# Two MoE layers on one core: the down biases move from matmuls to the copy out of PSUM, the first seventeen expert tiles take rounded products, and every engine's order is new

## Chip, cores and metric
The kernel runs on one core of one Trainium2 chip. The metric is device time in microseconds (us). Before the change the median of three runs is 795.2 us (793.75 to 796.96).

## What is computed
The input is x of 16 sequences of 256 rows of 128. Layer 0 is attention with 16 heads of 8, and then a mixture of experts. Layer 1 is a gated recurrence with a gated hidden layer, and then a channel mix. The change is in the mixture of experts, which is, with xf the 4096 rows:

```python
scores = jax.nn.sigmoid(xf @ gate_w + bias)
top_scores, top_idx = jax.lax.top_k(scores, 2)          # of 8 experts
top_scores = top_scores / (sum(top_scores) + 1e-06)
up = einsum('th,ehi->tei', xf, up_w) + up_b             # 128 -> 512
eo = einsum('tei,eih->teh', gelu(up), down_w) + down_b  # 512 -> 128
combined = einsum('teh,te->th', eo * 0.1, w)
shared = (gelu(xf @ sw_up + sb_up) @ sw_down + sb_down) * 0.1
out = shared + combined
out = out / (max(abs(out), -1) + 1e-06)
```

## The kernel before
The 4096 rows are eight chunks of 512. All engines run hand-ordered programs that meet at semaphores. `schedule()` (from L308) makes jobs, each a list of stages; two strings, ORDER1 and ORDER2, say in pairs of characters which job issues its next stage. `arrange` walks them, hands out the PSUM banks and buffers of the rings, and puts `fill` stages (short matmuls on constants, L855) where its model of costs (HELD, BEHIND, LANDS) finds TensorE idle too long. Each engine then issues its own stages in the order of the one list, and each waits in that order: what stands behind a waiting instruction waits too.

The work has four parts.
- **Attention**, chunks and sequences interleaved (ORDER1). Its stages among others: `mxm`/`mxr` (row maxima: TensorE L952, VectorE L1290), `atm` (L975, L977), `pv` (L990, L992). In it the layer norm and the routing of a chunk follow its attention, and GpSimd scatters the chunk's rows to the experts' places in HBM (`scatter`, L1935, four stages a chunk; each waits until the one before has landed).
- **First list** (ORDER1): 17 tiles of 256 rows of one expert, which the routing of six chunks already fixes. SyncE's `fetch` reads the tile's expert and row from a table into registers and issues three DMAs, up weights WU (L2044), down weights WD (L2045) and rows XT (L2049), into one of six buffers; from the seventh tile it waits for the last down product of the tile six back. TensorE transposes the rows (`xt`, L1065), VectorE copies them to XS (L1517), four `up` products in float32 follow (L1079; one float32 product is two instructions in the trace), ScalarE's gelu (L1784), four `down` stages of two products each (L1098), VectorE's copy out `ev` (L1539), and GpSimd's `store_rows` (L1946).
- **Second list** (order written out in `schedule`): 22 tiles. VectorE rounds WU to float32r (`wsh`, L1528) and GpSimd takes the rest (`wsl`, WO, L1941); VectorE makes XH and XL of the rows likewise (L1519, L1521). An `up` is then three float32r products WH·XH, WO·XH, WH·XL (L1085 to L1087).
- **Last part** (ORDER2): GpSimd gathers each chunk's two rows per token (`gather`, L1963, each stage after the landing of the one before), VectorE combines (`cmb`, L1548), normalizes (`fin1`, L1570), TensorE transposes (`fin2`, L1113), and layer 1 follows for all chunks interleaved. The shared expert's `up` and `down` for chunk 0 stand at the start of the first list, those of chunks 1 to 7 here.

The down biases are applied with the shared expert's product: `rows` transposes each chunk's routing weights with a column of ones (TensorE L1057, four products; ScalarE L1772 copies them to WT), and the shared expert's last `down` adds four products of WT with the nine bias rows DB (L1105). `ev` of the shared expert (L1535) copies the sum out.

Of the kernel before, what the change touches and what calls it, by code (L numbers as in the profile page):

```python
# [7 lines left out]
F = mybir.dt.float32  # L8
R = mybir.dt.float32r
B16 = mybir.dt.bfloat16  # L10
ALU = mybir.AluOpType
# [27 lines left out]
def constants():  # L39
# [48 lines left out]
    "up": ("PE", 0.858, None), "rows": ("PE", 0.436, None), "down": ("PE", 0.888, None), "ev": ("DVE", 0.6, None),  # L88
    "gelu": ("ACT", 0.57, "gelu"), "t_up": ("PE", 0.434, None), "t_gelu": ("ACT", 0.36, "gelu"), "t_down": ("PE", 0.444, None),
    "t_ev": ("DVE", 0.33, None), "xt": ("PE", 0.218, None), "xs": ("DVE", 0.334, None), "store_rows": ("POOL", 0.55, None),  # L90
# [16 lines left out]
BEHIND = {"PE": 0.165, "ACT": 0.115, "DVE": 0.08, "POOL": 0.045, "SP": 0.0}  # L107
LANDS = {"gather": 2.5, "scatter": 2.5, "fetch": 3.0}
# [6 lines left out]
def cost(name, key):  # L115
# [7 lines left out]
    if name == "down" and key[0] == "s" and key[2] == 3:  # L123
        held = 1.776
# [6 lines left out]
    "AAAAACABAFAAABADAAAAABAEABAGAGABAAAAAKABALABAAAKAGALABAIAAAJAGAAAIAJAGAAABAHAAAIAGAHAGANAIAGAMANANABAMANAMAHABATAHAMABAP"  # L131
    "ATAHAPAQAGAQAHAOAHAOARASAHARAVBBAUASBABBApAoAXAYBABBAYAWBABBAWAYBDAYBAAXBEBDBCBEBFBCAXBFBGAXAWAXBGAWAZAXAWAZAYAWAZAsAZAY"
    "AZArAZArAtAaAqAtAqAcAbAcAtAsAhAbAiAsAtAqAqAhAtAtArAiAgArAhAqAgArAsAiAqAfAdAgAfAsArAGAdAsAfBHAuAHAIAdBHAwAeAwAGBIA1BJAGAv"
    "B1AIAvAIAkB1AIAeBNBKBNBLAkA1AeBKA0A0BNA1BNAyAjAkBLA0AyA2BNA2AjBNAyAzAjAxA2AzAmBcBdAlAmBLBKAlAzBMBLB1AnAxBKB1A4AnBMAIAnAx"
    "B3AnBMB3A4BMA3A4B4BKB4B5BKB5B6BMB6BLBMA3BLBgA3BfBfA6BhBOBeBhBQBgBQBPBeBVBWBVBPB0A6BWBSBVB0BSA5BWBUA5BfB0BhBfBSBTBUA7B0Bh"
    "BeBfA7BRBTBeA7BUBfB2BRA7BgBeBTB2B9BgA8BRBeBgB8BhBgAHBhBXA8BiBYBXAHBYBXAHBjBYBkBjA8BkCBA8BnBoCBCAB+A8B-CABaA8BnB-BoBZBnBq"
    "BaA-BqBZB-BoB+BpA-BmB-BpBbBqB+CABbB+CBBpBmBlCBCQBbCRBsCABmBlBbCpBsBlCpB+BsCAB+CBCpBrCACpB-CBCTBrB-CrBrCTCVCsCrCCBuCVCsCE"
    "CDCECtCDCUCtBuCJCICJCUCuCSCoCuCSCJCIA9CoCIBtCoA9CHA9BtCKCHCoCTA9BvCVBvCUCGCKCHCVCqCTCGBvCKCUCTCqCGCFBvCxCVCwCUCVBwCFCUCS"
# [171 lines left out]
def schedule():  # L310
# [126 lines left out]
    def plan(n):  # L437
# [3 lines left out]
        if n:  # L441
            yield stage("plan_rows", after=[("woh", NB - 1)])
# [48 lines left out]
    def shared_out(c):  # L491
        yield stage("ev", "s", c, after=[("down", "s", c, 3)])
# [1606 lines left out]
```

## Time and profile before

| | us |
|---|---|
| median of three runs | 795.2 |
| the profiled execution | 796.7 |
| its span in the trace | 795.0 |
| TensorE busy | 730.2 |
| VectorE busy | 502.4 |
| ScalarE busy | 498.3 |
| GpSimd busy | 387.8 |

The profile's mean granted TensorE clock is 0.971 of full speed. Starts and stretches in the text are us from the start of the span. By the trace the attention ends at about 360, the first list runs to 448, the second to 528, and the last part to the end. Matmul records overlap, since their ends are modelled: what a stage costs TensorE is read from start to start.

### The profile page before, as it was taken

What the parts mean: (1) busy time and instruction counts of PE and PEld (TensorE: products, weight loads), DVE (VectorE), ACT (ScalarE), POOL (GpSimd) and SP (SyncE); (2) the same over time, 40 slices, a digit from 0 to 9 for tenths busy, and PEclk for the clock granted to TensorE, in tenths of its full rate; (3) what the DMA queues carried; (4) which work ended last, traced back from release to release, by engine and by line L of the source; (5) the groups of instructions that cost most, each with busy time, mean ns of one, the idle gap of its engine ahead of it and who ended that gap; (6) DMA issues with size and microseconds to landing.
All of it is one profiled execution on the core that took longest, in us unless ns stands there. A gap on an engine that the chain in (4) does not pass through costs nothing.

```text
span 795.0 us, 12566 instructions
## 1 busy us (share of the span) xinstructions
PE 730.2 (92%) x3768; PEld 442.7 (56%) x3768; DVE 502.4 (63%) x1906; ACT 498.3 (63%) x749; POOL 387.8 (49%) x563
## 2 busy tenths in 40 slices
PE   4889899899889998988999899998999999999994
PEld 3444445444544544446789899986545644434442
DVE  3387888879984889784912345513346495795652
ACT  1749675775838556655455455552688886688563
POOL 7327444664856277653451355534445465522243
PEclk9999998999999989899999999998999999999998
DMA  9990000000000000005767667711000101000012
GB/s 280 380 369 29 1 1 0 18 12 14 14 24 4 2 28 24 3 15 168 231 214 214 179 204 233 208 40 31 26 25 23 31 22 32 20 1 0 1 40 66
DMA packets 59855, 64.18 MB, mean 81 GB/s; under 512 B 6474, under 2 KB 42668, under 8 KB 59788
## 3 DMA queue, kind: packets, MB, share of 16 engines
q1 hardware_dynamic: 53410, 49.84, 20.3%
q0 software_dynamic: 6320, 13.53, 5.4%
q8 instruction: 30, 0.49, 0.3%
q14 instruction: 37, 0.30, 0.1%
q10 hardware_dynamic: 58, 0.02, 0.0%
HBM read 35.18 MB, written 28.18 MB: 80 GB/s over the span
## 4 chain that ended last, share of the span: by engine, by line
PE 61%; DVE 15%; issue 8%; POOL 6%; ACT 6%; DMA 3%; SPq 0%; DVEq 0%; POOLq 0%; ACTq 0%
PE PS L1098 11%; DVE JK L1290 6%; PE PS L1079 4%; PE PS L952 3%; PE PS L990 3%; PE PS L1161 3%; PE PS L895 3%; PE PS L1154 3%; PE PS L1168 2%; PE PS L901 2%; POOL got L1963 2%; PE PS L907 2%; DMA got<-expert_out,IG 2%; PE PS L975 2%; PE PS L961 2%
## 5 line engine op out<-in xcount | busy, mean ns | idle before, releaser
L1290 DVE CUSTOM_DVE_ANT_0 JK<-PS,CM 128x256 bf16<-128x256 f32 (+1 forms) x512 | 148.9, 352 | 23.3 <-PE PS L952 21.9
L1784 ACT ACTIVATE GF<-PS,XN 128x256 f32<-128x256 f32 x156 | 73.7, 475 | 67.1 <-PE PS L1087 37.4
L1098 PE MATMUL PS<-WD,GF 128*128 128x128 f32 x624 | 94.9, 276 | 0.9 <-ACT GF L1784 0.6
L952 PE MATMUL PS<-KZ,QS 128*128 128x512 f32 x192 | 87.2, 506 | 5.5 <-DVE MX L1290 3.0
L1963 POOL DMA_INDIRECT got<-expert_out,IG x64 | 63.6, 993 | 54.4 <-DMA got<-expert_out,IG 38.2
L1098 PEld LDWEIGHTS PS<-WD,GF 128*128 128x128 f32 x624 | 85.9, 192 | 6.4 <-ACT GF L1784 1.9
L1935 POOL DMA_INDIRECT expert_rows<-five,IU x64 | 63.1, 986 | 50.2 <-DMA expert_rows<-five,IU 20.4
L1738 ACT ACTIVATE PA<-PS 128x1024 f32<-128x1024 f32 x64 | 64.1, 1029 | 21.7 <-PE PS L975 21.4
L1922 POOL TENSOR_SCALAR_AFFINE_SELECT PA<-PA 128x256 f32<-128x256 f32 x128 | 50.0, 420 | 52.1 <-ACT PA L1738 50.7
L1885 POOL TENSOR_SCALAR H<-xc,MOD 128x256 f32<-128x256 f32 x56 | 32.9, 598 | 79.4 <-DVE xc L1259 79.3
L952 PEld LDWEIGHTS PS<-KZ,QS 128*128 128x128 f32 x192 | 35.6, 197 | 43.9 <-DVE MX L1290 20.7
L1946 POOL DMA_DIRECT2D expert_out<-YT x39 | 21.7, 557 | 68.8 <-DVE YT L1539 68.1
L1922 POOL TENSOR_SCALAR_AFFINE_SELECT PB<-PB 128x512 f32<-128x512 f32 x64 | 39.5, 645 | 18.9 <-ACT PB L1740 18.7
L1290 DVE DVE_READ_ACCUMULATOR2_ANT MX<- 128x1 f32 x512 | 42.3, 83 | 0.0
L1079 PE MATMUL PS<-XS,WU 128*128 128x256 f32 x136 | 41.2, 385 | 1.0 <-DVE XN L1535 0.5
L1606 DVE SCALAR_TENSOR_TENSOR hf<-PS,V,GF 128x512 f32<-128x512 f32 x32 | 23.7, 745 | 28.1 <-PE PS L1161 25.4
L1098 PEld LDWEIGHTS PS<-five,GF 128*128 128x128 f32 x256 | 33.8, 196 | 11.8 <-issue 10.8
L1740 ACT ACTIVATE PB<-PS 128x1024 f32<-128x1024 f32 x32 | 32.5, 1027 | 7.2 <-PE PS L977 5.8
L895 PE MATMUL PS<-X,CT 128*128 128x512 f32 x64 | 35.4, 636 | 1.5 <-DVE X L1333 1.4
L901 PE MATMUL PS<-sq,CT 128*128 128x512 f32 x58 | 32.4, 644 | 4.4 <-DVE MX L1290 1.8
L990 PE MATMUL PS<-PA,VA 128*32 128x512 f32 x256 | 34.3, 629 | 2.2 <-DVE MX L1290 0.5
L1539 DVE COPY YT<-PS 128x256 f32<-128x256 f32 x39 | 16.5, 424 | 31.1 <-PE PS L1098 31.1
(295 smaller groups left out, 1741.6 us busy)
## 6 DMA issues: line engine op xcount, KB each, us to landing
expert_rows<-five SPq DMA_DIRECT2D x16, 1024.0 KB, 12.8
WU<-in_L_ffn_up_w SPq DMA_DIRECT2D x39, 256.0 KB, 2.9
WD<-in_L_ffn_down_w SPq DMA_DIRECT2D x39, 256.0 KB, 3.1
XT<-expert_rows SPq DMA_DIRECT2D x39, 128.0 KB, 3.2
expert_out<-YT POOLq DMA_DIRECT2D x39, 128.0 KB
PA<-in_L_attn_x SPq DMA_DIRECT2D x8, 256.0 KB, 5.5
out<-yo SPq DMA_DIRECT2D x8, 256.0 KB, 2.3
expert_rows<-five,IU POOLq DMA_INDIRECT x64
```

The source lines that it names most:

```text
L895: pe.matmul(bank("lc", c, s), centre, chunk(X, c), start=True, stop=True).then_inc(sems["cen"], 1)
L901: pe.matmul(bank("ln_var", c, s), mean, sq_of("sq", c, s), start=True, stop=True).then_inc(sems["var"], 1)
L952: pe.matmul(bk.rearrange("p (j n) -> p j n", n=wd), q, ks, start=True, stop=True).then_inc(sems["mx_mm"], 1)
L990: m = pe.matmul(o, VA[:, 2 * b % 8, j, :], p0[:, j, 2 * h:2 * h + 2, :], start=True, stop=False)
L1079: pe.matmul(bk[:, 0:TR], WU[u % NF][:, f], XS[slot["xs", u]][:, :], start=True, stop=True).then_inc(sems["up"], 1)
L1098: m = pe.matmul(bk[:, b], g[:, b], wd[:, k, :], start=(k == 0 and t == 0), stop=(k == 3 and t == TB - 1 and kind == "t"))
L1290: m = dve.tensor_tensor_reduce(JK[n % 2][:, s], bk[:, s], CM[:, 256 - wd:256] if wd == 128 else CM[:, 0:256], -1.0, 3.0e38, ALU.add, ALU.m ...
L1738: m = act.activation(PT0[b % 2][:, j:j + 2, g:g + 2, :].rearrange("p j g n -> p j (g n)"), two(both), ACT.Exp, scale=SCALE)
L1784: act.activation(GF[slot["gf", kind, u, k]][:, 0:n], bank("up", kind, u, k)[:, 0:n], ACT.Gelu, bias=bias).then_inc(sems["gelu"], 1)
L1922: m = pool.affine_select(out=a, in_=a, pattern=[[0, 2 if u < 4 else 4], [1, 128]], compare_op=ALU.is_ge, fill=zero, base=0, channel_multip ...
L1935: pool.indirect_dma_start(out=XD[:, :], out_offset=bass.IndirectOffsetOnAxis(ap=IU[:, c, n, k:k + 1], axis=0), in_=HT[c % 2][:, k, :], in_ ...
L1963: pool.indirect_dma_start(out=got[b][n][:, k, :], out_offset=None, in_=YD[:, :], in_offset=bass.IndirectOffsetOnAxis(ap=IG[:, n, 4 * c + k ...
```

## The change
1. The stage `rows`, the buffers WT and DB and the four bias products at the end of each shared `down` are gone. A tile's `fetch` issues a fourth DMA, the expert's down bias broadcast to 128 partitions into BD (ahead of XT), and waits for the `ev` of the tile six back in place of its last `down`. `ev` adds BD, or for the shared expert SD, to the PSUM bank as it copies.
2. The tiles of the first list go the way of the second: XH and XL, `wsh` and `wsl` before each, three float32r products an `up`.
3. ORDER1 and ORDER2 are replaced; a few costs of the model are other numbers, the buffers of the output are freed in it by the store, and the last step of the routing plan also waits for the last chunk's routing weights.

```diff
-BEHIND = {"PE": 0.165, "ACT": 0.115, "DVE": 0.08, "POOL": 0.045, "SP": 0.0}
-LANDS = {"gather": 2.5, "scatter": 2.5, "fetch": 3.0}
+BEHIND = {"PE": 0.25, "ACT": 0.12, "DVE": 0.08, "POOL": 0.045, "SP": 0.0}
+LANDS = {"gather": 2.5, "scatter": 2.5, "fetch": 3.0, "store": 2.0}
...
-                        + ([("down", "t", t - NF, 3)] if t >= NF else []))
+                        + ([("ev", "t", t - NF)] if t >= NF else []))
...
+    def tile_weights(t):
+        yield stage("wsh", t, takes=[(WS2, "ws", (t,), ("up", "t", t, 3))], after=[("fetch", t)] + ([("wsh", t - 1)] if t else []))
+        yield stage("wsl", t)
...
-                if k == 1:
-                    yield stage("rows", c, takes=[(ring, "rows", (c,), ("rw", c)), (WTS, "wts", (c,), ("down", "s", c, 3))])
...
-                if u < N1:
-                    pe.matmul(bk[:, 0:TR], WU[u % NF][:, f], XS[slot["xs", u]][:, :], start=True, stop=True).then_inc(sems["up"], 1)
-                    return
...
-            if kind == "s" and k == 3:
-                w.wait_ge(*at("rw", u))
-                w.wait_ge(ld_db, 32)
-                for t in range(4):
-                    b = slice(128 * t, 128 * t + 128)
-                    m = pe.matmul(bk[:, b], WT[slot["wts", u]][:, b], DB[:, :], start=False, stop=(t == 3))
...
-            if t < N1:
-                dve.tensor_copy(XS[slot["xs", t]][:, :], a).then_inc(sems["xs"], 1)
-                return
...
-                dve.tensor_copy(chunk(XN, u), bank("down", kind, u)).then_inc(sems["ev"], 1)
+                w.wait_ge(ld_sd, 16)
+                dve.tensor_tensor(shared(u), bank("down", kind, u).rearrange("p (k d) -> p k d", d=128),
+                                  SD[:, :].unsqueeze(1).to_broadcast([128, 4, 128]), ALU.add).then_inc(sems["ev"], 1)
...
-            dve.tensor_copy(YT[u % 3][:, :], bank("down", kind, u)[:, 0:TR]).then_inc(sems["ev"], 1)
+            dve.tensor_tensor(YT[u % 3][:, :].rearrange("p (k d) -> p k d", d=128),
+                              bank("down", kind, u)[:, 0:TR].rearrange("p (k d) -> p k d", d=128),
+                              BD[u % NF][:, :].unsqueeze(1).to_broadcast([128, TB, 128]), ALU.add).then_inc(sems["ev"], 1)
...
             if t >= NF:
-                w.wait_ge(*at("down", "t", t - NF, 3))
+                w.wait_ge(*at("ev", "t", t - NF))
...
+            sp.dma_start(BD[k][:, :], i["L0_ffn_down_b"][bass.ds(ex, 1)].rearrange("o h -> (o h)").partition_broadcast(128)
                          ).then_inc(ld_t[k], 16)
```

What the new strings say, read as stages (beside what the old ones say):
- SyncE: fetch 0, 1, 3, 2, 5, 4, 8, 6, 7, 9 and so on (before 1, 0, 5, 2, 3, 4, 6, 7, 8, 9).
- GpSimd from chunk 6's scatter on: scatter 6 0; wsl 0; wsl 1; scatter 6 1; scatter 6 2; wsl 2; wsl 3; wsl 4; scatter 6 3; store_rows 0, 1, 2; wsl 5; scatter 7 0; store_rows 3; wsl 6, ending with scatter 7 3 ahead of wsl 12.
- ScalarE: the exponential of chunk 6's routing stands ahead of the second norm of chunk 7, not behind it. The order makes 65 changes of the activation table (73 before).
- TensorE: the first list's interleaving of `up` and `down` is near the old one. In the last part `fin2` of chunk 0 comes after 13 shared `up` and 9 shared `down` stages (12, and 8, before). Up to the last output projection of the attention it changes 221 times between the three kinds of step `atm`, `pv` and the rest (198 before).
- Fills: 10 stages with 27 products in all (35 stages with 50).

## Rows read from the trace of the kernel before

**Rows 1.** The page: the chain that ended last, by engine
```profile
PE 61%; DVE 15%; issue 8%; POOL 6%; ACT 6%; DMA 3%; SPq 0%; DVEq 0%; POOLq 0%; ACTq 0%
```

**Rows 2.** Busy time (instructions) by stretch: PE, PEld, DVE, ACT, POOL, clock, DMA
```profile
0.00:360.00 360.00, 319.39 (x1718) 166.28 (x1719) 278.80 (x1420) 229.12 (x330) 202.27 (x353) 0.96 0.20 67
382.80:448.30 65.50, 64.25 (x442) 57.79 (x441) 23.91 (x71) 32.31 (x68) 20.78 (x28) 1.00 0.71 215
459.50:518.00 58.50, 58.50 (x515) 58.50 (x514) 28.88 (x68) 32.32 (x69) 31.78 (x35) 1.00 0.73 220
552.30:760.00 207.70, 204.18 (x637) 102.17 (x638) 129.10 (x240) 155.96 (x201) 90.30 (x100) 0.98 0.07 18
```

**Rows 3.** TensorE in order of time: two transposes of the first list, two of the second
```profile
405.40 0.38 PE L1065 MATMUL PS<-CT,XT 128*128 128x128 f32 x2
...
409.13 0.38 PE L1065 MATMUL PS<-CT,XT 128*128 128x128 f32 x2
...
459.52 0.38 PE L1065 MATMUL PS<-CT,XT 128*128 128x128 f32 x2
...
462.95 0.38 PE L1065 MATMUL PS<-CT,XT 128*128 128x128 f32 x2
```

**Rows 4.** VectorE in order of time: a rounding that meets GpSimd's, and one that doesn't
```profile
449.98 1.38 DVE L1528 CAST WH<-WU 128x512 fp32r<-128x512 f32 x1
...
454.24 0.43 DVE L1528 CAST WH<-WU 128x512 fp32r<-128x512 f32 x1 [0.47 <-PE PS L1087]
```

**Rows 5.** Groups by line: a copy, an operation of its size, the rest of WU
```profile
L1535 DVE COPY XN<-PS 128x512 f32<-128x512 f32 x8 | 5.5, 684 | 17.4 <-PE PS L1105 17.4
L1259 DVE TENSOR_TENSOR xc<-PS,rs 128x512 f32<-128x512 f32 x22 | 15.0, 687 | 23.6 <-ACT rs L1673 23.6
L1941 POOL TENSOR_TENSOR WO<-WU,WH 128x512 fp32r<-128x512 f32 x22 | 28.5, 1294 | 2.8 <-DVE WH L1528 2.5
```

**Rows 6.** SyncE's queue in order of time: DMA issues of the first fetches
```profile
371.93 0.34 SPq L2044 DMA_DIRECT2D WU<-in_L_ffn_up_w  x1
...
372.97 0.35 SPq L2049 DMA_DIRECT2D XT<-expert_rows  x1
374.65 0.33 SPq L2044 DMA_DIRECT2D WU<-in_L_ffn_up_w  x1
```

**Rows 7.** TensorE in order of time, shared expert: a transpose of weights, a last down
```profile
529.73 0.60 PE L1057 MATMUL PS<-CT,WS 128*9 128x128 f32 x4
530.17 1.88 PE L1075 MATMUL PS<-H,five 128*128 128x512 f32 x4
531.89 1.05 PE L1098 MATMUL PS<-five,GF 128*128 128x128 f32 x8
532.78 1.02 PE L1075 MATMUL PS<-H,five 128*128 128x512 f32 x2
...
537.58 1.05 PE L1098 MATMUL PS<-five,GF 128*128 128x128 f32 x8
538.57 1.15 PE L1105 MATMUL PS<-DB,WT 9*128 9x128 f32 x8
539.65 1.13 PE L1075 MATMUL PS<-H,five 128*128 128x512 f32 x2
```

**Rows 8.** The page, DMA issues: KB each, median us from issue to landing
```profile
XT<-expert_rows SPq DMA_DIRECT2D x39, 128.0 KB, 3.2
```

**Rows 9.** GpSimd in order of time: scatters of chunk 6
```profile
379.60 0.96 POOL L1935 DMA_INDIRECT expert_rows<-five,IU  x1 [3.18 <-DMA expert_rows<-five,IU]
...
385.48 1.09 POOL L1935 DMA_INDIRECT expert_rows<-five,IU  x1 [3.66 <-DMA expert_rows<-five,IU]
```

**Rows 10.** TensorE in order of time: first up of tile 2
```profile
387.95 0.67 PE L1079 MATMUL PS<-XS,WU 128*128 128x256 f32 x2
```

**Rows 11.** TensorE at chunk 0's transpose
```profile
552.34 1.12 PE L1113 MATMUL PS<-CT,on 128*128 128x128 f32 x4 [2.84 <-DVE on L1570]
```

**Rows 12.** By stretch, columns as rows 2: a fall of the clock in attention
```profile
128.00:140.00 12.00, 9.82 (x23) 4.70 (x22) 9.61 (x41) 6.67 (x11) 5.45 (x11) 0.72 0.00 1
```

More of the change, by code:

```diff
@@ L135 @@
[L135 to L138, printed above, removed]
@@ L193, in frees @@
         for n, k in enumerate(self.ids):
-            ends = [done.get((SIGNALS[s], *key)) for s, *key in self.ends.get(k, ())]
+            ends = [done.get((SIGNALS.get(s, s), *key)) for s, *key in self.ends.get(k, ())]
             if None not in ends:
@@ L298 @@
     "pl_ei": "plan_tiles", "pl_ub": "plan_bias", "pl_ix": "plan_rows", "pl_w": "plan_rows",
-    "rw_tp": "rows", "rw": "rows", "xt_tp": "xt", "xs": "xs", "w_hi": "wsh", "w_lo": "wsl", "up": "up", "gelu": "gelu", "down": "down", "ev": "ev",
+    "xt_tp": "xt", "xs": "xs", "w_hi": "wsh", "w_lo": "wsl", "up": "up", "gelu": "gelu", "down": "down", "ev": "ev",
     "cmb": "cmb", "fin": "fin1", "fin_bk": "fin2", "moe_x": "fin3", "cen": "lc",
@@ L441, in plan @@
         if n:
-            yield stage("plan_rows", after=[("woh", NB - 1)])
+            yield stage("plan_rows", after=[("woh", NB - 1), ("rt_out", NCH - 1)])
     def fetches(n):
@@ L488, in shared_units @@
                 yield stage("down", "s", c, k, takes=[(ring, "down", ("s", c), ("ev", "s", c))] if k == 0 else [],
-                            after=[("gelu", "s", c, k)] + [("load_late",)] * (k == 3))
+                            after=[("gelu", "s", c, k)])
     def shared_out(c):
-        yield stage("ev", "s", c, after=[("down", "s", c, 3)])
+        yield stage("ev", "s", c, after=[("down", "s", c, 3), ("load_late",)])
     for l in range(2):
@@ L602, in channel @@
         yield stage("om", c, takes=[(BK, "o_bk", (c,), ("yo", c))])
-        yield stage("yo", c, takes=[(YO, "yo", (c,), ("yo", c))])
+        yield stage("yo", c, takes=[(YO, "yo", (c,), ("store", c))])
         yield stage("store", c)
@@ L1049, in dpm @@
             m.then_inc(sems["dp_mm"], 1)
-        def rows(c):
-            w.wait_ge(*at("wst", c))
-            w.wait_ge(zeroed, 4)
-            for e in prior["rows", c]:
-                w.wait_ge(*at(*e))
-            for k in range(4):
-                m = pe.transpose(bank("rows", c)[0:9, 128 * k:128 * k + 128], WS[:, c, k, :], ident)
-            m.then_inc(sems["rw_tp"], 1)
         def xt(t):
-            w.wait_ge(ld_t[t % NF], 48 * (t // NF + 1))
+            w.wait_ge(ld_t[t % NF], 64 * (t // NF + 1))
             for e in prior["xt", t]:
@@ L1201, in tensor @@
               "pjm": pjm, "spm": spm, "vm": vm, "mxm": mxm, "qmt": qmt, "atm": atm, "pv": pv, "nrt": nrt, "stt": stt, "wom": wom,
[L1202 removed]
+              "rtm": rtm, "htt": htt, "dpm": dpm, "xt": xt, "up": up, "down": down, "fin2": fin2, "tw": tw,
               "zd": zd, "yam": yam, "ym": ym, "fam": fam, "fm": fm, "mom": mom, "km": km, "rm": rm, "v1m": v1m, "om": om}
```

130 lines of the change are left out of this document (62 added, 68 removed).

## Prediction
> **What bounds it now.** I read the chain that ended last first: TensorE carries 61% of it [rows 1]. Then the table by stretch, to see where TensorE is really full [rows 2]: in the second list 58.50 of 58.50 us, in the first 64.25 of 65.50, in the last part from 552.30 to 760.00 204.18 of 207.70, all at or near full clock. There, product time taken away is time. The attention is another thing: TensorE 319.39 and VectorE 278.80 of 360 us, clock 0.96; neither fills it, and waits from one to the other make up the rest. Last I read TensorE in order of time, for what one stage costs from start to start.
>
> **First list, products.** From transpose to transpose a tile of the first list takes 409.13 - 405.40 = 3.73 us; one of the second, which already multiplies in three rounded parts, 462.95 - 459.52 = 3.43 [rows 3]. 17 tiles x 0.30 = 5.1 us less.
>
> What a tile adds off TensorE: on VectorE a rounding of the weights (0.43) [rows 4] and a second pass over the rows (about as long, my estimate from the first, which reads as many PSUM columns), so some 15 us beside 23.91 busy in 65.50 [rows 2]; on GpSimd the rest of the weights, 17 x 1.29 = 21.9 us [rows 5] beside 20.78 [rows 2]. Both engines have the room, and two buffers let it be done a tile ahead. If that cover is gone, the tile's `up` waits for its rest; that is priced below. `ev` with an addition costs what the copy costs: 0.687 beside 0.684 for 512 columns [rows 5]. Nothing for it.
>
> The fourth DMA: two issues of SyncE span 372.97 - 371.93 = 1.04 us, so 0.5 for one more; a whole fetch takes 374.65 - 371.93 = 2.72 [rows 6]. It becomes 3.2, still under a tile's 3.43. In bytes, 64 KB come to the 768 that a tile reads and writes (256, 256, 128 and 128), which lifts the DMA share of 0.73 [rows 2] to about 0.79. Waiting for `ev` and not for the last `down` makes a fetch some 0.6 us later (a copy of 0.4 and the hops), and it is made six tiles ahead. I cost all this at nothing. What covers it is the lead of six tiles; where the order spends that lead, at tile 6, it counts (next part).
>
> **Chunk 0 and the start of the list.** A `rows` stage holds TensorE 530.17 - 529.73 = 0.44 us. A last shared `down` with the biases takes 539.65 - 537.58 = 2.07, an ordinary one 532.78 - 531.89 = 0.89, so the biases cost 1.18 [rows 7]. For chunk 0 that is 1.6 us less. Fetch 0 ahead of fetch 1 lands the first tile up to 2.7 us earlier [rows 6], and the routing of chunk 6 comes earlier on ScalarE.
>
> But GpSimd now has two scatters in a row ahead of tile 2's rest. `wsl` 1 can't run before fetch 1 has landed. The second fetch of the old kernel issues its rows at 372.97 [rows 6]; with the broadcast ahead about 373.5, landed 3.2 later [rows 8], 376.7; rounding and rest 1.7: 378.4. Then a scatter (two instructions of 1 us and 0.3 between, 2.3), its landing (GpSimd idled 3.18 and 3.66 us for it) [rows 9], say 3.4, a scatter 2.3, and `wsl` 2, 1.3: 387.7, and a hop. The old kernel began tile 2 at 387.95 [rows 10]. So the head start and the 1.6 us end in one wait for GpSimd, of up to 3 us. Fetch 8 now goes ahead of 6 and waits for tile 2's `ev`, so that fetch 6 is issued about 6 us after it could be: 0 to 2 us at tile 6. Against that stands what the old list loses at its own start. I take 0 for this part, with ends of -4 (no such wait) and +4 (both waits, and the clock falling after them).
>
> **Last part.** Seven `rows` and seven bias groups go: 7 x (0.44 + 1.18) = 11.3 us. Three `rows` and two bias groups of them (3.7 us) stood before chunk 0's `fin2`, where TensorE then waited 2.84 us for the gather and combination [rows 11]. That chain (store, four gather stages, combination, norm) is untouched, so their time only becomes more waiting. The new order puts one more `up` (1.72 us for two, 530.17 to 531.89, so 0.86) and one more `down` (0.89) into it [rows 7]: 1.75 won back. What comes off behind it is 4 x 0.44 + 5 x 1.18 + 1.75 = 9.4 us, in a stretch that is full [rows 2]. ScalarE also loses its copies to WT and some table loads; it wasn't the bound, so nothing.
>
> **Attention.** No product changes, only the order. The whole kernel has 23 fill products fewer, at 0.22 each (a quarter of a `down`) [rows 7], at most -5.1, if every one delayed something. TensorE changes 23 times more between kinds of step; no row prices that alone, and I bound it by nothing and by the same 0.22, +5.1. What can be more is the clock: from 128 to 140 it was 0.72 of full, so 12 x 0.28 = 3.4 us of work lost, with 9.82 of 12 us busy [rows 12]. Five such falls lose some 13.5 us by the same sum. I take -1; the ends are -13 (all falls gone) and +8 (more changes and one or two more falls).
>
> **Sum.** On the profiled execution's 796.7 us: -5.1 + 0 - 9.4 - 1 = -15.5, so 781.2. That execution is 1.5 us above the median of 795.2, against which it is 779.7. I say 780.
>
> **A rule against the change.** A rounding of WU on VectorE that started while GpSimd's subtraction ran took 1.38 us and not 0.43 [rows 4]. It is one of 22 in the second list; were it one of 22 in the first too, that is under 1 us, off the path. There GpSimd also scatters, at shifting phases, so more of the 17 may meet. The Trainium skill, page "SBUF — State Buffer", section "SBUF: two separate sides", says that VectorE in a two-port mode and GpSimd take a shared port pair in turn, each for a whole instruction while the other stands still; by that rule, read for every tile, the sum would lose what the third rival below loses. The trace agrees for the one rounding that met.
>
> **Rivals.**
> - *The new attention order keeps the clock up.* For: 13.5 us lie there. Against: fewer fills also keep TensorE less busy. Half of the falls gone and a little of the fills: another -8, 772.
> - *The last part doesn't take it.* For: its chain also goes through GpSimd (6%) and DMAs (3%) [rows 1], so TensorE may wait where it now computes. Against: 204.18 of 207.70. If 2 of the 9.4 us arrive, 788.
> - *Roundings held up.* All 17 meet GpSimd, and each delay of 0.95 us [rows 4] stands on TensorE's path: +16, 796, no change. Against: one in 22 so far, and a tile of lead.
> - *Slower: the rests queue behind the scatters.* Place: GpSimd in the first list, where eight scatter stages of chunks 6 and 7 stand between the `wsl`. A tile's `up` needs its own rest. Two buffers give one tile of lead, 3.43 us less rounding and rest, 1.7. A scatter that must wait for a landing holds GpSimd 3.4 + 2.3 = 5.7; a full hit costs 5.7 - 1.7 = 4 us. Four hits eat the gain, five to eight end above the old time: eight, 812. For: the waits of rows 9. Against: the order mostly puts a `wsl` into the landing, and all but a few rests have a scatter behind them and not ahead.
> - *It doesn't do what it says*: the three rounded products run in the second list at the price used [rows 3], so I give this nothing.
>
> **Chances.** Forecast 0.55; clock 0.20; last part 0.13; roundings 0.05; scatters 0.05; 0.02 for a gain of a kind that I don't see. A measurement of this kernel can tell about 0.5%, 4 us: faster is under 791.2, slower over 799.2. Faster: 0.53 of the forecast, 0.20, 0.10 and 0.02, so 0.85. Same: 0.02 of the forecast, 0.03 of the last part's, 0.03 of the roundings', so 0.08. Slower: 0.02 of the roundings' and 0.05, so 0.07. The range takes the forecast with the ends of the list's start, the clock rival for the most part and the last part's: 769 to 790. Outside are the roundings, the scatters, and a clock that hardly falls.
>
> **What would show it.** Right: 3.43 us from transpose to transpose in the first list; no L1057 and no L1105; TensorE's wait before chunk 0's `fin2` at 4 to 5 us and the stretch behind it 9 us shorter at the same busy share; tile 2 beginning as long after the end of attention as it did, with a wait for WO before it. Wrong: waits for WO at several tiles with a fallen clock behind each; roundings of 1.4 us in number; an attention over 5 us shorter or longer; TensorE's busy share in the last part well under 0.98; tiles waiting for BD.

## The result, and the profile after

The changed kernel takes 775.0 us (median of four runs, 772.8 to 776.4) where the kernel before took 795.96 beside it: ratio 0.974, with an interval of 0.970 to 0.977. The forecast was 780.0, the range 769 to 790. The profiled execution took 776.25 us, its span is 774.2.

The size is right and its make-up is not. I split both spans at the same five events of TensorE:

```
stretch of the span                                  before   after   change   forecast
start to the last output projection                  359.79  343.88   -15.9    -1
last projection to the first up of tile 17            91.4   100.1    +8.7     -5.1, and 0 for the start
tile 17 to the first shared up of chunk 1             76.8    77.9    +1.1      0
from there to chunk 0's transposes (fin2)             24.3    24.2    -0.1      0
from there to the end                                242.7   228.1   -14.5     -9.4
```

Three stretches of the kernel after, busy time by engine in the columns of [rows 2]:

```profile
0.00:343.90 343.90, 307.69 (x1680) 158.42 (x1680) 285.46 (x1420) 226.93 (x329) 204.68 (x355) 0.98 0.21 71
358.00:444.00 86.00, 74.38 (x569) 70.46 (x569) 50.80 (x133) 36.19 (x77) 46.65 (x49) 0.94 0.65 193
546.10:774.20 228.10, 214.82 (x652) 106.42 (x652) 144.69 (x266) 159.31 (x216) 107.73 (x118) 0.98 0.09 25
```

The middle row is the one to read first. The first list held TensorE 64.25 of 65.50 us before [rows 2]; now TensorE is busy 74.38 of 86 and its clock is 0.94. Where it waits stands in TensorE's order of time (in brackets the idle time and what ended it):

```profile
343.88 0.68 PE L1016 MATMUL PS<-ST,wo 128*128 128x256 f32 x2
...
357.99 0.69 PE L1055 MATMUL PS<-CT,XT 128*128 128x128 f32 x2 [4.47 <-DMA XT<-expert_rows]
...
375.95 0.58 PE L1072 MATMUL PS<-XH,WH 128*128 128x256 f32 x1 [2.55 <-DVE XL L1500]
...
392.99 0.55 PE L1072 MATMUL PS<-XH,WH 128*128 128x256 f32 x1 [4.15 <-issue]
...
411.73 0.38 PE L1055 MATMUL PS<-CT,XT 128*128 128x128 f32 x2
...
415.17 0.38 PE L1055 MATMUL PS<-CT,XT 128*128 128x128 f32 x2
...
418.93 0.39 PE L1072 MATMUL PS<-XH,WH 128*128 128x256 f32 x1 [0.17 <-DVE YT L1520]
419.39 0.38 PE L1055 MATMUL PS<-CT,XT 128*128 128x128 f32 x2
...
423.62 0.38 PE L1055 MATMUL PS<-CT,XT 128*128 128x128 f32 x2
...
443.97 0.55 PE L1072 MATMUL PS<-XH,WH 128*128 128x256 f32 x1 [1.71 <-POOL WO L1916]
...
546.08 0.54 PE L1094 MATMUL PS<-CT,on 128*128 128x128 f32 x2 [4.80 <-DVE on L1553]
```

The instruction behind each of the four long waits is slow, 0.69 us for the transposes' 0.38, and 0.55 to 0.58 for an up's first product, 0.36 in a steady tile: TensorE had stood idle, and the granted clock was 0.50 of full (356 to 360, 376 to 378, 393 to 395, 444 to 446), the lower of its two levels, 1.2 GHz in place of 2.4. From transposes to transposes the steady tiles take 3.44, 4.22 and 4.23 us by turns, not 3.43. VectorE's order of time tells what two of the long waits are:

```profile
351.30 0.15 DVE L1376 TENSOR_TENSOR IU<-s,m 128x4 uint32<-128x4 f32 x1
358.06 0.43 DVE L1507 CAST WH<-WU 128x512 fp32r<-128x512 f32 x1 [6.61 <-DMA XT<-expert_rows]
358.40 0.18 DVE L1319 TENSOR_TENSOR rank<-PS,gbias 128x32 f32<-128x32 f32 x1
...
370.40 1.82 DVE L1412 TENSOR_TENSOR XN<-XN 128x7 f32<-128x7 f32 x1
...
375.47 0.42 DVE L1500 TENSOR_TENSOR XL<-PS,XH 128x256 fp32r<-128x256 f32 x1
...
385.00 1.54 DVE L1467 TENSOR_TENSOR R<-SL,XN 128x256 f32<-128x256 f32 x1
...
391.91 0.19 DVE L1490 TENSOR_TENSOR W<-sum,W 128x32 f32<-128x32 f32 x1
...
392.47 0.42 DVE L1500 TENSOR_TENSOR XL<-PS,XH 128x256 fp32r<-128x256 f32 x1
```

The added `wsh` 0 stands in VectorE's queue ahead of chunk 7's routing, and waits 6.61 us for tile 0's fetch; the routing's first step, whose product was long there, runs right behind it at 358.40. So the second plan of the tiles comes at 368.76 and tile 2's rows behind it. The plan of the rows, 385.00 to 392.10 in one piece, stands ahead of tile 5's rows: the 4.15 us that the trace puts down to "issue" end 0.1 us after XL is written. A difference of 7 columns took 1.82 us beside GpSimd's subtraction for tile 2 (370.90, 1.28 long), where such a difference takes 0.17.

SyncE's queue gives the 4.47 us at tile 0: between the last projection and fetch 0 it issues the eleven late loads. They are not new: twelve stood there before, and the first tile's rows were issued 10.1 us behind the last projection, 10.4 now. What is new is that TensorE has less to do in front of the tile: it comes to tile 0's transposes 14.1 us behind the projection, wait included, 16.3 before.

```profile
345.56 0.33 SPq L2001 DMA_DIRECT2D SD<-in_L_ffn_sb_down  x1
...
350.58 0.50 SPq L2008 DMA_DIRECT2D gates<-in_L_attn_w_out  x1
352.67 0.36 SPq L2018 DMA_DIRECT2D WU<-in_L_ffn_up_w  x1
...
354.31 0.33 SPq L2025 DMA_DIRECT2D XT<-expert_rows  x1
356.40 0.34 SPq L2018 DMA_DIRECT2D WU<-in_L_ffn_up_w  x1
```

Last the groups by line (the additions with the bias, the rests of WU, and the 512 row maxima of the attention with VectorE's idle time ahead of them), then that last group in the kernel before:

```profile
L1520 DVE TENSOR_TENSOR YT<-PS,BD 128x256 f32<-128x256 f32 x39 | 16.5, 424 | 32.0 <-PE PS L1085 32.0
L1916 POOL TENSOR_TENSOR WO<-WU,WH 128x512 fp32r<-128x512 f32 x39 | 50.3, 1289 | 32.5 <-DVE WH L1507 32.0
L1271 DVE CUSTOM_DVE_ANT_0 JK<-PS,CM 128x256 bf16<-128x256 f32 (+1 forms) x512 | 149.4, 351 | 13.1 <-PE PS L951 12.1
```

```profile
L1290 DVE CUSTOM_DVE_ANT_0 JK<-PS,CM 128x256 bf16<-128x256 f32 (+1 forms) x512 | 148.9, 352 | 23.3 <-PE PS L952 21.9
```

The 512 maxima take VectorE the same time to 1 us, and it waits 10 us less for their scores; all its 1,420 instructions of the attention keep it busy for longer, 285.46 us for 278.80 [rows 2]. "Clock loss" below is the sum over 4 us stretches of length times the withheld share of the clock: 13.7 us in the old attention, 6.8 in the new, 1.7 and 8.5 from there to the end of the second list, 4.3 and 1.7 from chunk 0's transposes to TensorE's last product.

### The profile page after: what moved, and what is told of

The parts are those of the page before. It is cut to its first block, busy times and chain, and to the rows that moved or that the text cites. A ratio compares the mean times of both kernels' runs of the same rounds, so it can differ in the third digit from the quotient of the medians.

```text
span 774.2 us, 12596 instructions
## 1 busy us (share of the span) xinstructions
PE 701.9 (91%) x3694; PEld 429.8 (56%) x3694; DVE 527.3 (68%) x1940; ACT 481.8 (62%) x733; POOL 411.1 (53%) x579
## 4 chain that ended last, share of the span: by engine, by line
PE 56%; DVE 22%; issue 8%; ACT 5%; DMA 4%; SPq 3%; POOL 2%; DVEq 0%; ACTq 0%; POOLq 0%
PE PS L1085 10%; DVE JK L1271 7%; PE PS L951 4%; PE PS L1135 3%; PE PS L894 3%; PE PS L1072 3%; PE PS L989 3%; PE PS L1149 3%; PE PS L1142 3%; PE PS L1073 2%; PE PS L1074 2%; PE PS L900 2%; PE PS L906 2%; PE PS L974 1%; PE PS L991 1%
## 5 line engine op out<-in xcount | busy, mean ns | idle before, releaser
L1085 PE MATMUL PS<-WD,GF 128*128 128x128 f32 x624 | 93.2, 277 | 0.0
L1085 PEld LDWEIGHTS PS<-WD,GF 128*128 128x128 f32 x624 | 82.5, 194 | 0.1
L1916 POOL TENSOR_TENSOR WO<-WU,WH 128x512 fp32r<-128x512 f32 x39 | 50.3, 1289 | 32.5 <-DVE WH L1507 32.0
L1072 PE MATMUL PS<-XH,WH 128*128 128x256 f32 x156 | 57.6, 369 | 10.9 <-issue 4.1
L951 PEld LDWEIGHTS PS<-KZ,QS 128*128 128x128 f32 x192 | 34.2, 189 | 48.7 <-issue 15.9
L1074 PE MATMUL PS<-XL,WH 128*128 128x256 f32 x156 | 45.0, 289 | 0.0
L1073 PE MATMUL PS<-XH,WO 128*128 128x256 f32 x156 | 45.0, 288 | 0.0
L1085 PEld LDWEIGHTS PS<-five,GF 128*128 128x128 f32 x256 | 35.7, 204 | 12.9 <-issue 12.7
L1498 DVE CAST XH<-PS 128x256 fp32r<-128x256 f32 x39 | 16.5, 423 | 37.4 <-PE PS L1055 37.1
L1072 PEld LDWEIGHTS PS<-XH,WH 128*128 128x128 f32 x156 | 31.0, 199 | 14.2 <-issue 5.9
L1520 DVE TENSOR_TENSOR YT<-PS,BD 128x256 f32<-128x256 f32 x39 | 16.5, 424 | 32.0 <-PE PS L1085 32.0
```

The source lines that it names most:

```text
L951: pe.matmul(bk.rearrange("p (j n) -> p j n", n=wd), q, ks, start=True, stop=True).then_inc(sems["mx_mm"], 1)
L1072: pe.matmul(bk[:, 0:TR], wh, xh, start=True, stop=False)
L1073: pe.matmul(bk[:, 0:TR], wo_, xh, start=False, stop=False)
L1074: pe.matmul(bk[:, 0:TR], wh, xl, start=False, stop=True).then_inc(sems["up"], 1)
L1085: m = pe.matmul(bk[:, b], g[:, b], wd[:, k, :], start=(k == 0 and t == 0), stop=(k == 3 and t == blocks - 1))
L1916: pool.tensor_tensor(WO[slot["ws", t]][:, :], WU[t % NF][:, :], WH[slot["ws", t]][:, :].bitcast(F), ALU.subtract).then_inc(sems["w_lo"], 1)
```

## The experiments

All are built from the changed kernel. The order strings don't show a move, so the diffs give them as the steps that they stand for. A change of order also changes, through the planner's model, which PSUM bank a step gets and how many filler matmuls (the `fill` stages) stand in the list; where that mattered it is said. The kernel before ran beside each group, at medians of 797 to 804 us with single runs from 792 to 811, so I judge by the stretches of the trace first:

```
run                         last        tile 0 to   tiles 8-16,   last part   ratio (interval)
                            projection  tile 17     each
before                      359.79      75.1        3.75          242.7       1
after                       343.88      86.0        4.00          228.1       0.974 (0.970-0.977)
e1 attention order          372.10      84.5        4.10          229.0       0.998 (0.990-1.007)
e2 last part order          347.27      87.1        4.10          235.7       0.986 (0.979-0.993)
e3 first list float32       344.63      79.3        4.06          228.9       0.963 (0.956-0.970)
e4 routing first            346.18      82.8        4.12          229.4       0.970 (0.964-0.977)
e5 old order, old banks     358.79      83.6        4.06          230.0       0.992 (0.983-1.000)
e6 rows' plan split         346.58      84.6        4.04          228.2       0.973 (0.966-0.980)
e7 fetch first              346.50      85.5        4.14          228.7       0.963 (0.955-0.970)
e8 fetch first, float32     346.70      77.7        4.06          229.3       0.959 (0.952-0.966)
e9 steady tiles old order   350.39      84.6        3.98          229.8       0.982 (0.978-0.986)
e10 regular list            346.14      78.7        3.95          228.4       0.962 (0.959-0.965)
e11 regular list, float32   347.20      72.7        3.78          229.8       0.954 (0.950-0.958)
e12 rows two ups early      348.28      76.0        4.03          229.4       0.966 (0.962-0.970)
```

**e1 and e5, the attention.** The steps ahead of the first shared up in the old order; e5 also with the old delay behind an engine's end:

```diff
-ORDER1, its first 1,424 steps as changed
+ORDER1, the same 1,424 steps in the order of the kernel before
...
-BEHIND = {"PE": 0.25, "ACT": 0.12, "DVE": 0.08, "POOL": 0.045, "SP": 0.0}
+BEHIND = {"PE": 0.165, "ACT": 0.115, "DVE": 0.08, "POOL": 0.045, "SP": 0.0}
```

(The second half in e5 alone.)

> The changed kernel with the 1,424 steps ahead of the first up product (all the attention and the first six chunks' routing) in the old order; everything behind them as changed. Theory (the new order of the attention took 15.9 us off, 359.79 to 343.88 at the last output projection): the last projection starts at 355 to 361 us again and the time is 788 to 793. Rival (the attention's gain was only a clock that happened to stay up, 13.7 us of clock loss against 6.8): the projection's time depends on where the granted clock falls, the clock loss of the attention stays near 7 us and the projection starts at 344 to 350, the time 775 to 781.

> As the run with the attention's old order, but with the planner's old delays behind an engine's end (0.165 and 0.115 us, not 0.25 and 0.12), so that the attention's steps, its PSUM banks and its filler matmuls are exactly those of the kernel before; from the last projection on all is as changed in order. Theory (the changed kernel's gain ahead of the tiles is the new order with the banks that belong to it): the last projection starts at 358 to 362 us as in the kernel before, the rest takes as long as in the changed kernel, ratio to the kernel before 0.985 to 0.995; the 12 us by which the old order with the new delays was late beyond that were banks. Rival (the change's other parts load the attention too, such as four transfers or the new tables): the projection starts at 365 us or later again.

e1 starts the last projection at 372.10, later than either side said, and took 801.6 us, level with the kernel before beside it. e5, whose attention is the old one step by step, bank by bank, filler by filler, at 358.79:

```profile
0.00:372.10 372.10, 328.49 (x1731) 173.50 (x1731) 282.21 (x1420) 229.19 (x330) 202.53 (x352) 0.95 0.19 65
```

```profile
0.00:358.80 358.80, 314.21 (x1718) 164.54 (x1718) 282.64 (x1420) 228.75 (x330) 202.78 (x352) 0.98 0.20 68
```

(The first fence is e1, the second e5.) e5 went as its theory said: the projection at 358.79, the ratio 0.992. With the new order and its banks taken back, the whole change is worth 0.8%, and its interval reaches to nothing. So that order is most of the result: 358.79 - 343.88 = 14.9 us by these two traces, and 0.992 - 0.974 of 796, some 14 us, by the runs.

Read the 14.9 with its spread. The changed kernel, e2 to e4 and e6 to e12 have the same attention, step for step, bank for bank and filler for filler, and their last projections start at 343.88 to 350.39, at 346.7 on the mean; the changed kernel's trace is the earliest of the eleven. The order with its banks is thus worth 8 to 15 us, 12 on the mean.

Part of that spread goes with the clock. The later starts have the larger clock loss: 343.88 with 6.8 us, 344.63 to 347.27 with 10.2 (six kernels), 346.50 to 350.39 with 13.7 (four). That is about 4 us at the end for 6.9 us of loss; the old attention's two traces show less, 359.79 with 13.7 and 358.79 with 6.8. Most of the gain is not the clock: at 6.8 us of loss the new order is 14.9 us ahead of the old, and at 13.7 it is 9.4 to 13.3 ahead.

Of the 14.9 us, 6.5 are TensorE's busy time (314.21 to 307.69), where the list of steps has 20 filler products and not 45 (these matmuls hold 8.0 us of the attention, 17.1 in e5); 8.4 are idle time. No run takes order, banks and fillers apart, so which of them gives the time stays open. e1 shows how much can hang on banks: the same order with other banks and 52 fillers ends 13.3 us later than e5, with a clock loss of 17.1, so that clock and banks are mixed in this pair too.

**e2, the last part.** ORDER2 as before, without its seven `rows` steps.

```diff
-ORDER2 as changed
+ORDER2 of the kernel before, less rows 1 to rows 7
```

> The changed kernel with the last part's steps in the old order, less the seven steps of the shared biases. The last part, from chunk 0's transposes behind the mixture to the end, fell from 242.7 to 228.1 us, 14.5, where my sum for the removed matmuls was 9.4. Theory: 9.4 is the matmuls and some 5 us is the new order; the last part takes 231 to 235 us, the time is 778 to 782. Rival: the new order does nothing and the removed matmuls are all of it (a higher clock with them): the last part stays at 227 to 229, time 774 to 777.

235.7 us for the last part, just above the theory's 231 to 235, and far from the rival's 227 to 229. The time, 789.0 us at a ratio of 0.986, isn't the 778 to 782 expected: in this run the attention ended at 347.27, tile 0 to tile 17 took 1.1 us more, and the kernel before ran at 803.0 us beside it, not at 796. Three kernels, the part behind chunk 0's transposes (the kernel before, e2; the changed one stands above):

```profile
552.30:795.00 242.70, 228.46 (x718) 113.75 (x718) 144.25 (x265) 172.41 (x227) 106.16 (x118) 0.97 0.08 24
```

```profile
551.20:786.90 235.70, 219.49 (x662) 107.05 (x662) 144.35 (x265) 170.24 (x223) 106.37 (x118) 0.98 0.09 25
```

Taking out the transposes and the bias products takes 228.46 - 219.49 = 9.0 us off TensorE's busy time, 1.6 of them clock (loss 4.3 to 2.7 up to TensorE's last product), and 7.0 off the stretch, because its idle time grows by 2. The new order takes another 4.7 of busy time and 2.9 of waits, 7.6 us. Of the 4.7, 1.75 are the `up` and the `down` that now stand ahead of the transposes (10 matmul instructions fewer, 662 to 652) and 1.0 is clock (loss 2.7 to 1.7).

**e3, the first list's product.**

```diff
             else:
                 w.wait_ge(*at("xs", u))
+                if u < N1:
+                    pe.matmul(bk[:, 0:TR], WU[u % NF][:, f], XS[slot["xs", u]][:, :], start=True, stop=True).then_inc(sems["up"], 1)
+                    return
...
-        jobs += [(0.0, j) for j in (tile_rows(t), tile_weights(t), tile_up(t), gelu("t", t), tile_down(t))]
+        jobs += [(0.0, j) for j in (tile_rows(t), tile_up(t), gelu("t", t), tile_down(t))]
```

> The changed kernel with the first list's first product in float32 again (one copy of the rows, no rounding of the weights for tiles 0 to 16), all other steps in the changed order; results of the first list are then those of the old product. Theory (the roundings' steps in VectorE's queue cost the list more than the three parts give: the wait of the rounding of tile 0's weights for its fetch holds chunk 7's routing for 6.6 us, and tiles 2 and 5 wait 2.55 and 4.15 us, with the clock down after each): PE has 5 us more to do but those two waits go, the stretch from the last projection to tile 17 falls from 100.1 to 91 to 97 us, the time is 766 to 773. Rival (the product is worth its 5.1 us and the waits come from GpSimd's scatters or the fourth transfer of each fetch): the stretch grows to 103 to 106 us, the time is 778 to 781.

The theory's side: 86.0 us from tile 0 to tile 17 become 79.3, and the waits at tiles 2 and 5 are gone, though TensorE has 5 us more to do. In this order the three-part product, with the roundings and rests that it brings, doesn't pay for itself. The steady tiles show something else: 4.06 us each with the old product, in the new order, where the old order has 3.75. So the new order of the list, with its banks, costs 0.3 us a tile by itself.

**e4, the queue behind `wsh` 0.**

```diff
-wsh 0, scatter 6 0, wsl 0, rtm 7, rtl 7, rt_sig 7, htt 7, hta 7, xt 0, xs 0, down s 0 0
+rtm 7, rtl 7, rt_sig 7, htt 7, hta 7, rt_cmp 7, rt_tie 7, rt_rank 7, dpm 7, rt_sum 7, dpd 7
+wsh 0, scatter 6 0, wsl 0, xt 0, xs 0, down s 0 0
...
-plan_tiles 1, scatter 6 1
+wsh 1, wsl 1, plan_tiles 1
```

> The changed kernel with chunk 7's routing and places (11 steps) ahead of the first rounding of a tile's weights, and the second plan of the tiles right behind the rounding of tile 1's weights. Theory (VectorE's queue order makes tile 2's wait): VectorE works during its idle 6.61 us, tile 2's wait of 2.55 us goes or is under 0.5 us, tile 5's wait behind the plan of the rows stays (2 to 4.2 us), the clock is lost once rather than twice; time 770 to 773. Rival (the wait is of GpSimd's, whose difference of the weights stands behind the scatters): tile 2 waits 2 us or more for WO, time 774 to 777.

Tile 2's wait of 2.55 us is gone, with GpSimd's order untouched: it was VectorE's queue, and neither the scatters nor WO. Tile 5's stays, and a smaller one is new, since TensorE now stands before the mask of chunk 7. In time it gave nothing that the runs can tell: the stretch from the last projection to tile 17 fell by 2.8 us, and the ratio, 0.970, can't be told from the changed kernel's 0.974.

```profile
360.03 0.19 PE L1044 MATMUL PS<-MASK,BEFORE 128*128 128x40 bf16 x1 [1.75 <-DVE MASK L1346]
...
391.47 0.35 PE L1072 MATMUL PS<-XH,WH 128*128 128x256 f32 x1 [3.96 <-DVE XL L1500]
```

**e6, the plan of the rows in three stages**, on top of e4.

```diff
-xs 4, plan_rows, xs 5, ev t 3, wsh 6, ev t 4, xs 6, wsh 7
+xs 4, plan_rows_a, xs 5, ev t 3, wsh 6, plan_rows, ev t 4, xs 6, wsh 7, plan_rows_w
```

> Chunk 7's routing ahead of the first rounding, as in the run before this one, and the plan of the rows (14 operations, 7.1 us in one piece) cut in three stages with tile 5's rows, tile 6's and tile 7's weights between them. Theory (tile 5's first up waited for its rounded rows behind the plan): the wait of 3.96 us goes and with it the fall of the clock at 392, the stretch from the last projection to tile 17 falls from 97.3 to 91 to 94 us, ratio 0.963 to 0.967. Rival (the wait was the fetch or the scatters, queued past their time): a wait of 2 us or more stands at tile 5 or 6 still, ratio 0.969 to 0.972.

The rival's outcome, ratio 0.973; of its path I had named one half in the forecast, fetch 6 behind fetch 8. XL of tile 5 is early now (387.25), but TensorE waits at tile 6 instead:

```profile
396.58 0.66 PE L1057 MATMUL PS<-CT,XT 128*128 128x128 f32 x2 [4.60 <-DVE YT L1525]
```

VectorE and GpSimd in this run:

```profile
389.55 0.42 DVE L1525 TENSOR_TENSOR YT<-PS,BD 128x256 f32<-128x256 f32 x1 [1.87 <-DMA expert_out<-YT]
394.08 0.43 DVE L1512 CAST WH<-WU 128x512 fp32r<-128x512 f32 x1 [4.11 <-DMA XT<-expert_rows]
...
396.02 0.41 DVE L1525 TENSOR_TENSOR YT<-PS,BD 128x256 f32<-128x256 f32 x1
```

```profile
382.46 1.01 POOL L1916 DMA_INDIRECT expert_rows<-five,IU  x1 [0.15 <-issue]
383.78 0.96 POOL L1916 DMA_INDIRECT expert_rows<-five,IU  x1 [0.30 <-issue]
384.75 1.70 POOL L1927 DMA_DIRECT2D expert_out<-YT  x3
```

Tile 3's `ev` needs the buffer that tile 0 stored from, and the stores of tiles 0 to 2 stand on GpSimd behind a scatter (here the queue I feared in the forecast does bite); then the rounding for tile 6 waits for fetch 6, queued on SyncE behind fetch 8, and tile 4's `ev` behind that. Both lay hidden behind the wait at tile 5.

**e7 and e8, fetches first**, with the split plan:

```diff
-load_late, fetch 0, fetch 1, fetch 3, fetch 2, fetch 5, fetch 4
+fetch 0, fetch 1, load_late, fetch 2, fetch 3, fetch 4, fetch 5
```

> The split plan, tiles fetched in rising order with the fetches of tiles 0 and 1 ahead of the eleven late loads on SyncE, chunk 7's comparisons behind the rounding of tile 1's weights and beside the shared expert's products, and the first three turns of late weights after tile 0. Theory (tile 0's 4.47 us wait for its rows is the 5.5 us of late loads ahead of it on SyncE): the first transposes of rows start at 353 to 355 us, 10 us behind the last projection and not 14, the stretch to tile 17 takes 86 to 90 us, ratio 0.952 to 0.960. Rival (what is gained at tile 0 is waited for again at tile 2, whose fetch is no earlier than before): the stretch takes 91 us or more, ratio 0.961 to 0.966.

> The same with the first list's first product in float32 (the weights' roundings of tiles 0 to 16 taken out, one copy of the rows; the results of the first list are then those of the old product). Theory (with its stalls mended the three-part product is worth the 5.1 us of TensorE's time that I gave it): 3 to 6 us slower than the run with the split plan and the early fetches. Rival (VectorE's and GpSimd's added work costs the list as much as TensorE saves, wherever it stands): within 2 us of it, or faster.

Tile 0's transposes come 9.5 us behind the last projection and not 14.1, without a wait: that half of the theory holds. From there to tile 17, though, e7 takes 85.5 us: TensorE waits 1.76 us for chunk 7's mask, and 2.90 and 1.28 for VectorE's `ev`, which waits for stores that stand behind the scatters. From the projection on that is 94.9 us and not 86 to 90, the rival's number, but not by the rival's cause, since no wait stands at tile 2. The float32 twin takes 77.7 from tile 0 to tile 17, and its time is 3.1 us shorter: e8 went to its rival.

**e9 to e12, the order of the list.** e9 puts the steps from tile 8's rows on back in the old order; e10 writes the whole list in one regular order, and e11 is e10 in float32:

```diff
-xt 10, down 9 0, down 9 1, up 10 0, down 9 2, up 10 1, down 9 3, up 10 2, xt 11, down 10 0, up 10 3
+xt 10, up 9 3, down 9 2, up 10 0, down 9 3, up 10 1, down 10 0, up 10 2, down 10 1, xt 11, up 10 3
```

> The changed kernel with the first list from tile 8's rows on in the old order (an up, a down, an up, a down; the weights' roundings of the next tile behind a tile's first up), nothing else moved. In the changed kernel tiles 8 to 16 come every 3.44, 4.22 and 4.21 us by turns, 3.96 on the mean, where the second list has 3.43 and the old list 3.73. Theory (the searched order costs it: an up product takes a PSUM bank that the eviction has only just left, and two downs stand at once): tiles come every 3.43 to 3.5 us, the stretch from the last projection to tile 17 falls from 100.1 by 3 to 5 us, ratio 0.966 to 0.970. Rival (four PSUM banks in place of eight, or the roundings beside scatters and stores on GpSimd, hold the first list): tiles take 3.8 us or more on the mean, ratio 0.972 to 0.975.

> The run with the early fetches, and the whole first list in the regular order: one up, one down, each tile's store on GpSimd ahead of the next scatter, one scatter in two tiles, tile 17's weights rounded beside tile 16 in the buffers that tile 15 left. Theory (nothing in the three-part product is slow, only the queues around it): no wait over 1 us between tile 1 and tile 18, tiles every 3.43 to 3.5 us from tile 6 on, the stretch from the last projection to tile 17 takes 78 to 84 us, ratio 0.940 to 0.951. Rival (GpSimd's difference of the weights, 1.28 us a tile beside scatters of 2.3 and stores of 0.57, doesn't fit in 3.43 us): waits for WO or for the stores stand at tiles 5 to 12, the stretch takes 86 us or more, ratio 0.954 or above.

> The same with the first list's first product in float32 (results of the first list are then those of the old product). Theory (0.30 us a tile, 17 tiles: the three-part product is worth 5 us once nothing waits): tiles every 3.73 us, 4 to 6 us slower than the run beside it. Rival (as the pair before showed, where float32 was 7.7 us faster to tile 17): no slower than the run beside it.

e9: 3.98 us a tile, not 3.43. The rival has it. As a whole e9 is slower than the changed kernel, 0.982 for 0.974 with the intervals apart, though its list is 1.6 us shorter: its attention, the same steps, took 350.39, 6.5 us more, at 13.7 us of clock loss for 6.8. Why it differs so is open. e10: the long waits are down to 1.92, 1.12 and 0.92 us, 78.7 us from tile 0 to tile 17, but nearly every steady tile still takes 3.9. From the projection on the list takes 88.2 us and the ratio is 0.962, so both went to the rival. Waits for WO or the stores at tile after tile, as the rival had them, don't show. The trace shows another place (TensorE, one tile and the group behind it):

```profile
416.56 0.38 PE L1066 MATMUL PS<-CT,XT 128*128 128x128 f32 x2
416.70 0.36 PE L1083 MATMUL PS<-XH,WH 128*128 128x256 f32 x1
...
417.13 0.61 PE L1096 MATMUL PS<-WD,GF 128*128 128x128 f32 x4
417.92 0.39 PE L1083 MATMUL PS<-XH,WH 128*128 128x256 f32 x1 [0.17 <-DVE XL L1514]
...
418.37 0.61 PE L1096 MATMUL PS<-WD,GF 128*128 128x128 f32 x4
418.74 0.36 PE L1083 MATMUL PS<-XH,WH 128*128 128x256 f32 x1
...
420.46 0.38 PE L1066 MATMUL PS<-CT,XT 128*128 128x128 f32 x2
```

From a down's four matmuls to the next up it is 0.37 us where nothing waits (418.37 to 418.74), here 0.79 (417.13 to 417.92). The idle time is counted from the modelled end of the four, 0.61 us after their start, and where nothing waits the next group starts 0.24 us ahead of that end: the wait costs this overlap besides the 0.17 shown. XL, the second of two operations of VectorE behind the transposes, is written 1.30 us after their start (388.65 to 389.95 at an earlier tile), and the order leaves it two groups. e11, whose rows are one copy, has no such wait, and its tiles take what its theory said:

```profile
415.92 0.38 PE L1067 MATMUL PS<-CT,XT 128*128 128x128 f32 x2
...
419.65 0.38 PE L1067 MATMUL PS<-CT,XT 128*128 128x128 f32 x2
```

3.73 us a tile, but 6.0 us less than e10 to tile 17 and not 4 to 6 more; ratio 0.954 beside 0.962 with the intervals apart. That is the fastest of these kernels: 760.2 us beside 797.1, and below the changed kernel's 0.974 too, again with the intervals apart; its results of the first list are those of the product before.

e12 asks whether the wait for XL was all.

```diff
-                    after=[("fetch", t)] + ([("up", "t", t - 1, 2)] if t else []))
+                    after=[("fetch", t)] + ([("up", "t", t - 1, 1)] if t else []))
...
-up 9 2, down 9 1, xt 10, up 9 3, down 9 2, up 10 0
+xt 10, up 9 2, down 9 1, up 9 3, down 9 2, up 10 0
```

> The regular list with the three-part product, and: each tile's rows turned one up product earlier (behind the second up of the tile before, which the planner's rule kept behind the third), so that the copy and the difference on VectorE, 1.30 us from the transposes' start, have four matmul groups of 0.44 us ahead of the tile's first up and not two; chunk 7's places 1 us later on TensorE; the second plan of the tiles in two stages; no filler matmuls behind the attention. Theory (the regular list took 3.90 us a tile because tile t's first up waited for its difference of the rows, 0.18 us shown and about as much again in the empty pipeline): tiles 7 to 15 come every 3.43 to 3.5 us, the stretch from the last projection to tile 17 takes 78 to 83 us where the float32 twin took 82.2, ratio 0.946 to 0.954. Rival (four PSUM banks and VectorE's load hold the list at 3.9 us whatever the order): 3.75 us or more a tile, the stretch takes 86 us or more, ratio 0.959 or above.

It wasn't, and the rival's numbers hold: 88.4 us from the projection on, ratio 0.966. The wait for XL is gone from the steady tiles, some of them take 3.48 to 3.50 us, and others 4.3 and 4.9: the mean is 4.03. TensorE in the middle of a tile:

```profile
407.96 0.71 PE L1101 MATMUL PS<-WD,GF 128*128 128x128 f32 x4 [0.19 <-ACT GF L1793]
408.88 0.36 PE L1088 MATMUL PS<-XH,WH 128*128 128x256 f32 x1 [0.21 <-POOL WO L1949]
```

Now it is the activation in one place and GpSimd's rest of the weights in the next. Which of GpSimd's scatters and stores, and of the four PSUM banks that the first list shares (the second has eight), sets the limit was not separated; the theory that a better place for the rows gives 3.43 in every tile falls.

## Why the forecast was right, and which of its steps were not

*Attention, -1.* The step that failed most, and it carried the result: 15.9 us. I had read that VectorE is busy 278.80 of 360 us [rows 2] and that the rest is waits, and then priced only fillers, changes of step and clock; the waits themselves I priced at nothing. e5 puts 14.9 us on the new order with its banks, 12 on the mean of the eleven kernels that have it: 6.5 in TensorE's busy time, with half of the filler products gone, and 8.4 in idle time. The bound of 0.22 us for a change of step and for a filler didn't hold a term of this size. The clock's part came half true. The loss that I had summed as 13.5 us is 13.7, and it fell to 6.8, half of the falls gone, which is the condition of the first rival. But the rival gave this 8 us less than the forecast, and the same halving in the old order moved the end by 1.0 us, in the new one by about 4. So its cause was there and is the smaller part of the gain.

*First list, -5.1.* Failed, with the wrong sign: with the start of the list, which I took at 0, it is +8.7. The 3.43 us was read in the second list [rows 3] and carried over as if the product alone made it. The sum held for TensorE's work (the second list and every undisturbed tile say so), but the list's limit moved: 4.00 us a tile. e3 and e11 say what the product is worth here: -6.7 and -6.0 us if it is taken out again, roundings and rests with it.

*"What a tile adds off TensorE ... I cost at nothing."* By busy time the two engines had the room, and 39 rests of WU at 1289 ns [rows 5] show the durations right. What I left out is the queue: one `wsh` waiting 6.61 us for a DMA held the routing of another chunk. I looked for the held queue on GpSimd; it stood on VectorE, as e4 shows. The rival "the rests queue behind the scatters" had the wrong engine, and its mechanism came true only for the stores, once e6 had cleared the wait in front of them.

*The start of the list, 0 with ends of -4 and +4.* The size just holds: tile 2 began 32.1 us behind the last projection, 28.2 before [rows 10], +3.9. But its parts are others than mine. TensorE waits 4.47 us for fetch 0, which stands behind the late loads on SyncE and which I had not counted; tile 2's wait is the routing's and not GpSimd's; tile 6 doesn't wait, and tile 5 waits 4.15 us behind the plan of the rows.

*Fetch 3.2 us:* 3.22 from fetch 1 to the next (356.40 to 359.62), 3.7 for the first; but the rows land 3.8 us after their issue at the median, not 3.2 [rows 8]. *The addition as a copy:* 424 ns, as the copy. *The wait before chunk 0's `fin2`, 4 to 5 us:* 4.80, for 2.84 before [rows 11]; the time removed ahead of it became waiting. *BD:* no tile waited for it.

*Last part, -9.4.* Near for what it priced. By my prices the transposes and bias products behind chunk 0's `fin2` are 7.7 of the 9.4; e2 takes 7.0 off the stretch. The new order brings another 7.6, of which I had counted the 1.75 of one `up` and one `down`; of the rest, 1.0 is clock and 2.9 are waits.

*The rule against the change.* I had weighed one rounding that met GpSimd, 1.38 us [rows 4], and the page "SBUF — State Buffer" of the Trainium skill, section "SBUF: two separate sides", which tells of a port pair that the two engines hold in turns. Of the 39 roundings one met a subtraction of GpSimd again (443.09, tile 17's: 1.02 us for 0.43). Stretched were small steps of the routing and the plans: beside a subtraction 1.38 us for 0.42 (361.83), 1.82 for 0.17 (370.40) and 1.37 for 0.42 (387.38), and beside a scatter and the stores 1.54 for 0.41 (385.00). On the path this can have cost 1.65 us ahead of tile 2 and 2.1 ahead of tile 5, not the 16 of the rival: the trace agrees with the rule at the four places where a subtraction was met, and not at every tile.

So two errors of opposite sign met: the list is 13.8 us over its terms (+8.7 for -5.1), attention and last part 20.0 under theirs. That the sum came out within 5 us is luck.

## What to carry to other kernels

When work moves to an engine that has idle time, look for what stands behind it in that engine's queue: a step that waits for a DMA holds everything behind it (6.61 us here), and the busy shares don't show it. A time per tile belongs to its surroundings (banks, the other queues, how many groups lie between producer and user); carried from one stage to another, the 3.43 us was no more than a lower bound here. And measure the parts of a change apart even if the sum fits: here the three-part product, the change's centre, is 6 us slower in the list than the old one in the same regular order, and the best part of the gain came from an order that wasn't about the product at all. Set such a part beside the spread of kernels that share it: eleven runs of one and the same attention ended up to 6.5 us apart.

## What the runs showed that I had not expected

- A wait that the trace shows as 0.17 us before a matmul cost 0.42 us of the tile (0.79 for 0.37 from one group to the next, in e10), because the idle time counts from a modelled end that the next group otherwise overlaps; at one such wait a tile that is more than the 0.30 us that the product was to gain.
- The same 1,422 steps of the attention, with the same banks and fillers, ended at 343.88 to 350.39 us in eleven kernels, later as a rule where more clock was lost (6.8 us in the earliest, 13.7 in the latest). In the old order 13.7 and 6.8 us of loss made 359.79 and 358.79.
- The same order of the same steps with other PSUM banks and a few fillers more moved the last projection from 358.79 to 372.10, with a clock loss of 17.1 us for 6.8.
- The list's long waits lay one behind another. e4 took one away and gained 2.8 us in the list, e6 took the next and lost 2.0 again, because another stood behind each (3.96 us in e4, 4.60 in e6); e10, which left none over 1.92, gained 7.3 from tile 0 to tile 17.
